# A graph network on one core: the scatter's one-hot over 128 nodes instead of 256, with messages doubled and masked by node half

## The chip, the cores and the metric

The program runs on one core of a Trainium2 chip. That core has TensorE (matmuls, with its weight loads shown apart as PEld), VectorE (DVE), ScalarE (ACT), GpSimd (POOL) and SyncE (SP), which mostly issues transfers. The metric is the device time of one execution in microseconds (us); lower is better.

## The reference

Four message-passing layers over a graph of 50,000 nodes and 50,000 edges, sorted by destination, with 64 features. Each layer gathers rows by `src` (and by `dst`), makes a message for each edge, and sums the messages into the nodes by `dst`:

```python
# layer 0: gated edges
z = concatenate([x[dst], x[src], edge_attr]); m = sigmoid(z @ W_f + b_f) * softplus(z @ W_s + b_s) * gate
out = segment_sum(m, dst) + x
# layer 1: a two-layer network on each edge
m = relu(concatenate([h[src], h[dst], e]) @ W1 + b1) @ W2 + b2;  h_new = segment_sum(m, dst)
# layer 2: two attention layers with 5 heads
out = segment_sum(a[:, :, None] * xl[src], dst).mean(heads) + bias     # a: softmax over the edges of a node
# layer 3: copied rows
agg = segment_sum(h[src], dst) * deg_in ** -0.5;  h = elu(batchnorm(agg @ W + b))
```

`deg_in` is the number of edges that end in a node. It is used by layer 3, and in the attention layers to find nodes without edges.

## The kernel before

Edges are cut into 392 tiles of 128 (one edge a partition), and four tiles make a block: `BLK = 4`, `NB = 98` blocks. Since edges are sorted by destination, the nodes of a tile nearly always lie in a window of two node tiles (`WIN = 2`, 256 nodes); the few others are left to `extra_pass`, which reads the messages back from `m_d` in DRAM.

Five stages scatter messages: `gated_edges` (names end in `_e`, from 284 to 880 us), `plain_edges` (`_e`, 1065 to 1610 us), `attention_messages` twice (`_m`, 2558 to 2898 and 4002 to 4336 us) and `copied_edges` (`_e`, 4809 to 5312 us). All use the class `NodeSums`. For a block n:

- `hot` (ScalarE, lines 933 and 938) writes a one-hot matrix of each tile: 128 edges by 256 nodes, as relu(1 - |rel - iota|). In `gated_edges` two of the four tiles are made by `match` on VectorE (line 944).
- `multiply` (TensorE, line 956) makes two products a tile, one for each node half w: a one-hot of 128 edges by 128 nodes is the stationary operand, and the messages `m`, padded with zeros from 64 to `MOVED = 128` columns, are the moving one. Each f32 product stands in the trace as two records, so a block has 16. They go to two PSUM tiles: `part_0` for tiles 0 and 1 of the block, `part_1` for 2 and 3. There is one such pair for all blocks, so the products of block n wait until VectorE has added those of block n - 1, pair by pair: `need(pe, self.added, BLK * (n - 1) + t + 2)`.
- `add` (VectorE, line 973) adds each tile's two halves to the sums in `acc`, at a tile read from `lo_i`. The windows of two tiles can overlap, so each add waits for the one before it.

The order of the work is written out by hand: each engine has a `body(n, u, i)`, and the calls in it, with their lags, are that engine's order. Blocks 0 to 5 are written out, then a loop of four blocks a turn runs. No scheduler is in between; each engine runs in order and waits at semaphores.

`attention_messages`: TensorE's body n is `project(n)` (line 2218; two halves q of a block, each 4 records, into `xl`; the two bodies share the `xl` slot of the second half) and then the scatter of block n - 2. VectorE's body n is `weigh(n)` (line 2257, two instructions of 640 elements that multiply `xl` by the attention) and then `add(n - 2)`. GpSimd sums the heads of block n in three instructions (lines 2277, 2280, 2284) and so writes `m`. ScalarE's body makes the one-hots and copies the weights `als` into `m`.

`gated_edges`: TensorE's body n is `turn(n)` (lines 1094, 1289, 1100: transposes of the gathered rows and products that pick the rows of `dst`), the scatter of block n - 2 and `project(n)` (lines 1301 to 1308). ScalarE's body n copies what `turn(n)` left (lines 1345, 1347), runs the gates of block n - 1 (lines 1353 to 1363) and its one-hots. VectorE's body n is `near.hot(n)` (line 1083, a one-hot of the other direction), `add(n - 4)`, `message(n - 2)` and `finish_message(n - 2)` (lines 1406 and 1413, which write `m`), and `match(n - 1)`.

`plain_edges` has the lags 2 for the scatter and 3 for the adds, writes `m` on VectorE (line 1617, with the bias `b1b`), and counts the in-degrees: a 65th column of ones in `m`, and a second add of two elements a tile (line 976). In these two stages and in `copied_edges` GpSimd issues one indirect gather for each tile (lines 1059, 1195, 1657), into rings of four blocks. `copied_edges` only gathers rows `z` and scatters them; its VectorE first clears the padding of `z` (line 1685) and `acc` (line 1687).

## Time and profile before

| | us |
|---|---|
| median of 3 runs | 5562.61 (5561.23 to 5564.41) |
| the profiled execution's own time | 5557.08 |
| its span in the trace | 5555.0 |
| PE busy | 4095.7 (74%) |
| PEld busy | 3075.3 (55%) |
| DVE busy | 3270.0 (59%) |
| ACT busy | 2967.9 (53%) |
| POOL busy | 3265.0 (59%) |
| granted TensorE clock, mean | 0.871 of full speed |

The program is a row of stages with a barrier after each, and each stage has its own limit, so the shares over the whole span say little. In a stage the same body runs 98 times, and what matters is the distance from one block to the next. In a view of the order of time, the first number is the start and the second how long the merged group ran; "x16" is the number of records, and the bracket tells how long the engine sat idle before and what released it.

### The profile page before, as it was taken

The numbers are of one execution on the slowest core, as the hardware profiler recorded it, in microseconds if no ns is written. First come the engines' busy times: TensorE is split into PE (matmuls) and PEld (weight loads), VectorE is DVE, ScalarE is ACT, GpSimd is POOL, SyncE is SP. The second block draws the span as 40 slices with busy tenths as digits, with TensorE's granted clock in tenths as the row PEclk, the third lists the DMA queues.
The fourth block names the chain that finished last, engine by engine and source line by source line (L and its number), as shares of the span: only waits on it lengthen the run. The fifth ranks groups of instructions, "written<-read, shape, count | busy, mean of one in ns | idle before, by whom it ended". The sixth has DMA issues, their size and how long they took to land. (4 is left out here: it accounts for less than half of the span.)

```text
span 5555.0 us, 125887 instructions
## 1 busy us (share of the span) xinstructions
PE 4095.7 (74%) x31967; PEld 3075.3 (55%) x31967; DVE 3270.0 (59%) x7378; ACT 2967.9 (53%) x7228; POOL 3265.0 (59%) x3335
## 2 busy tenths in 40 slices
PE   1079996499961999975997679999299894155574
PEld 0068885487751666653773256666177552155552
DVE  3945557588876333337879943333688799622266
ACT  0268885466655555534872234555288324755547
POOL 0876662377732655525878965554188687677710
PEclk6589998799985999987999989999699997577785
DMA  9477774755547555541334455555133334622224
GB/s 256 87 168 179 179 180 101 155 155 154 152 121 204 123 120 120 120 98 53 121 106 95 95 132 120 120 121 122 33 121 121 90 92 96 142 78 79 79 65 145
DMA packets 1204167, 680.39 MB, mean 122 GB/s; under 512 B 625921, under 2 KB 1100477, under 8 KB 1202266
## 3 DMA queue, kind: packets, MB, share of 16 engines
q1 hardware_dynamic: 1039724, 532.72, 37.1%
q0 software_dynamic: 63360, 65.01, 7.0%
q10 hardware_dynamic: 100948, 81.22, 4.6%
q8 instruction: 42, 0.69, 0.1%
q14 instruction: 93, 0.76, 0.0%
HBM read 379.93 MB, written 298.10 MB: 122 GB/s over the span
## 5 line engine op out<-in xcount | busy, mean ns | idle before, releaser
L1989 DVE COPY zT_l<-zTp_l 128x512 f32<-128x512 f32 x196 | 135.5, 691 | 899.6 <-PE alp_l L1907 650.8
L933 ACT ACTIVATE hot_e<-iota_n,rel 128x256 f32<-128x256 f32 x980 | 422.8, 499 | 418.3 <-PE part_e L956 412.4
L973 DVE TENSOR_TENSOR acc<-acc,part_e 128x128 f32 x1176 | 335.2, 285 | 467.5 <-PE part_e L956 341.7
L1964 ACT ACTIVATE leak_l<-tp_l,bcat 128x512 f32<-128x512 f32 x588 | 375.9, 686 | 433.0 <-PE tp_l L1919 404.0
L956 PE MATMUL part_e<-z_e,hot_e 128*128 128x128 f32 x1568 | 282.4, 354 | 384.0 <-DVE acc L1687 187.0
L1059 POOL DMA_INDIRECT z_l<-h_d,src_i x392 | 384.1, 980 | 288.2 <-PE zTp_l L1100 192.1
L1059 POOL DMA_INDIRECT z_l<-g_d,src_i x392 | 384.6, 981 | 287.1 <-PE zTp_l L1100 190.9
L1969 ACT ACTIVATE leak_l<-tp_l,bcat 128x256 f32<-128x256 f32 x784 | 307.7, 476 | 345.1 <-PE tp_l L1926 345.1
L1059 POOL DMA_INDIRECT z_e<-h_d,src_i x392 | 377.9, 964 | 183.8 <-issue 96.8
L956 PEld LDWEIGHTS part_e<-z_e,hot_e 128*128 128x128 f32 x1568 | 260.2, 259 | 406.1 <-DVE acc L1687 187.2
L1195 POOL DMA_INDIRECT z_e<-h_d,row_of_e x392 | 384.7, 981 | 124.6 <-issue 113.1
L1657 POOL DMA_INDIRECT z_e<-h_d,src_i x392 | 370.0, 944 | 139.9 <-issue 90.5
L956 PEld LDWEIGHTS part_m<-m_m,hot_m 128*128 128x128 f32 x3136 | 365.5, 192 | 87.9 <-DVE acc L973 80.6
L956 PE MATMUL part_e<-m_e,hot_e 128*128 128x128 f32 x3136 | 393.8, 279 | 25.7 <-DVE acc L973 21.0
L956 PE MATMUL part_m<-m_m,hot_m 128*128 128x128 f32 x3136 | 402.7, 282 | 2.3 <-ACT m_m L2243 2.0
L956 PEld LDWEIGHTS part_e<-m_e,hot_e 128*128 128x128 f32 x3136 | 372.3, 191 | 53.1 <-DVE acc L973 39.2
L933 ACT ACTIVATE hot_m<-iota_n,rel 128x256 f32<-128x256 f32 x784 | 334.3, 497 | 108.2 <-PE part_m L956 106.7
L1919 PE MATMUL tp_l<-zT_l,wcat 128*128 128x256 f32 x1176 | 372.6, 399 | 14.9 <-DVE zT_l L1989 14.9
L1919 PE MATMUL tp_l<-zT_l,wswap_l 128*128 128x256 f32 x1176 | 351.6, 381 | 0.0
L2257 DVE TENSOR_TENSOR prod_m<-xl_m,al 128x640 f32<-128x640 f32 x392 | 304.9, 819 | 32.3 <-PE xl_m L2218 19.2
L2480 DVE TENSOR_TENSOR prod_a<-xl_a,wself_a 128x640 f32<-128x640 f32 x392 | 303.6, 814 | 30.8 <-PE xl_a L2374 30.2
L2374 PE MATMUL xl_a<-wl,hT_a 64*128 64x320 f32 x1568 | 292.4, 471 | 10.8 <-DVE prod_a L2480 0.5
(419 smaller groups left out, 11050.9 us busy)
## 6 DMA issues: line engine op xcount, KB each, us to landing
m_d<-m_e ACTq DMA_DIRECT2D x196, 256.0 KB, 2.2
m_d<-m_m SPq DMA_DIRECT2D x196, 256.0 KB
h_d<-h SPq DMA_DIRECT2D x56, 448.0 KB
relb_e<-rel_d SPq DMA_DIRECT2D x196, 128.0 KB
near_e<-h_d SPq DMA_DIRECT2D x392, 64.0 KB
near_e<-g_d SPq DMA_DIRECT2D x392, 64.0 KB
relb_l<-rel_d SPq DMA_DIRECT2D x196, 128.0 KB, 3.4
near_l<-h_d SPq DMA_DIRECT2D x392, 64.0 KB
```

Of the source, the lines that this page charges most:

```text
L933: ins = self.nc.scalar.activation(self.hots[k][:, t, :], self.S["iota_n"][:, :], ACT.Abs, scale=-1.0, bias=self.S["rel"][:, ds(n * BLK + t ...
L956: mm = self.nc.tensor.matmul(self.parts[t // 2][:, t % 2, w, :], self.hots[k][:, t, w * P:(w + 1) * P], m[:, t, :], start=True, stop=True)
L973: ins = self.nc.vector.tensor_tensor(x, x, part[:, t % 2, :, 0:x.shape[2]], ALU.add)
L1059: self.nc.gpsimd.indirect_dma_start(out=self.z[n % RINGS][:, t, SIDES[t % 2]], out_offset=None, in_=self.table[0:(TILES + 1) * P, :], in_o ...
L1195: self.nc.gpsimd.indirect_dma_start(out=self.z[n % RINGS][:, t, :], out_offset=None, in_=self.source[:, :], in_offset=bass.IndirectOffsetO ...
L1657: nc.gpsimd.indirect_dma_start(out=z[k][:, t, 0:C], out_offset=None, in_=S["h_d"][0:(TILES + 1) * P, :], in_offset=bass.IndirectOffsetOnAx ...
L1919: mm = nc.tensor.matmul(by_side(tp[q])[:, side], left[:, q, :], by_side(zT[k])[:, side], start=True, stop=True)
L1964: nc.scalar.activation(leak[u % 2][:, q, :], tp[q][:, :], ACT.Relu, bias=bcat[:, 0, q:q + 1], scale=1.0 - SLOPE).then_inc(leak_ready, 1)
L1969: nc.scalar.activation(by_side(leak[u % 2][:, 3 + q, :])[:, side], tp[3 + side][:, q * 2 * P:(q + 1) * 2 * P].rearrange("p (r e) -> p r e" ...
L2257: nc.vector.tensor_tensor(heads[:, 2 * q:2 * q + 2], xl[slot(u, q)][:, :, 0:HC].rearrange("p t (h c) -> p t h c", h=H), wide(al[:, ds(n * ...
L2374: mm = nc.tensor.matmul(xl[slot(u, q)][:, half, 0:HC], hT[u % 2][rows, q * P:(q + 1) * P], wl[rows, :], start=True, stop=True)
L2480: nc.vector.tensor_tensor(prod[k][:, 2 * q:2 * q + 2, :].rearrange("p t (h c) -> p t h c", h=H), xl[slot(u, q)][:, :, 0:HC].rearrange("p t ...
```

## The change

What it does, part by part:

- The one-hots are 128 edges by 128 nodes: `rel` is reduced modulo 128 in `setup`, and `part_of` (0 or 1 for each edge and node half) is kept beside it. `hot` and `match` write half as much; `match` is one TENSOR_TENSOR of 256 elements instead of two TENSOR_SCALARs of 256. The ring of one-hots has four entries (two in `gated_edges`).
- A new VectorE instruction, `pick`, writes the messages twice, once for each node half, multiplied by `part_of`: `split`, 4 tiles x 2 x 64 = 512 elements. In `attention_messages` it does three of the four tiles (420 elements in the first layer, 414 in the second), and ScalarE does the fourth with two small instructions (`pick_too`).
- `multiply` makes one product a tile: one-hot stationary, `split` moving (128 columns; 140 and 138 in the attention layers), so 8 records a block. It waits for `picked` where it waited for `m`.
- In `attention_messages` VectorE's body n is now `pick(n - 2)`, `weigh(n)`, `add(n - 3)`. In `gated_edges` `pick(n - 2)` comes last. In `plain_edges` ScalarE writes `m` (`take`), the bias comes in by a bf16 product of 256 columns, and `pick` stands where the message was. In `copied_edges` VectorE picks block n and adds block n - 1.
- `m` has no padding: `m_d` gets 64, 69 or 70 columns a message instead of 128.
- The in-degrees ride as a 70th column of ones in the first attention layer's messages (`AW = 70`) and are copied out in `attention_nodes`; the column and the second adds of `plain_edges` are gone.
- `setup` has three more VectorE instructions for `rel` and `part_of`, and 13 more for the bias rows `b1b3`. `finish` keeps its output buffers in the unused end of `acc`.

```diff
 class NodeSums:
-        self.hots = [... sbuf_tensor(f"hot_{name}_{k}", [P, BLK, WIN * P], F32) for k in range(2)]
+        self.hots = [... sbuf_tensor(f"hot_{name}_{k}", [P, BLK, P], F32) for k in range(deep)]
+        self.split = [... sbuf_tensor(f"split_{name}_{k}", [P, BLK, WIN, width], F32) for k in range(2)]
         self.parts = [... psum_tensor(f"part_{name}_{k}", [P, 2, WIN, MOVED], F32) for k in range(2)]
...
+    def pick(self, dve, n, u, m):
+        tiles = slice(0, self.picked_first)
         need(dve, self.summed, BLK * (n - 1))
-        for t in range(self.on_act, BLK):
-            ins = self.nc.vector.tensor_scalar(self.hots[k][:, t, :], self.S["iota_n"][:, :], self.S["rel"][:, ds(n * BLK + t, 1)], None, ALU.is_equal)
-        ins.then_inc(self.matched, 1)
+        self.nc.vector.tensor_tensor(self.split[u % 2][:, tiles, :, :], wide(m[:, tiles, :], 2, WIN),
+                                     wide(self.S["part_of"][:, ds(n * BLK, self.picked_first), :], 3, self.width), ALU.mult).then_inc(self.picked, 1)
...
-    def multiply(self, pe, n, k, m):
+    def multiply(self, pe, n, u):
         need(pe, self.hot_ready, n + 1)
+        pe.wait_ge(self.picked, n + 1)
         for t in range(BLK):
             if t % 2 == 0:
                 need(pe, self.added, BLK * (n - 1) + t + 2)
...
-            for w in range(WIN):
-                mm = self.nc.tensor.matmul(self.parts[t // 2][:, t % 2, w, :], self.hots[k][:, t, w * P:(w + 1) * P], m[:, t, :],
-                                           start=True, stop=True)
+            mm = self.nc.tensor.matmul(self.parts[t // 2][:, t % 2, :, 0:self.width], self.hots[u % self.deep][:, t, :], self.split[u % 2][:, t, :, :],
+                                       start=True, stop=True)
             if t % 2:
                 mm.then_inc(self.summed, 2)
...
 def attention_messages(nc, S, g):
...
                 def body(n, u, i):
+                    if has(n, 2):
+                        pick(n - 2, u + UN - 2)
                     weigh(n, u)
-                    if has(n, 2):
-                        sums.add(dve, n - 2, sums.windows(dve, n - 2))
+                    if has(n, 3):
+                        sums.add(dve, n - 3, sums.windows(dve, n - 3))
...
 def gated_edges(nc, io, S):
...
                     if has(n, 1):
-                        sums.match(dve, n - 1, (u + 1) % 2)
+                        sums.match(dve, n - 1, u + UN - 1)
+                    if has(n, 2):
+                        pick(n - 2, u + UN - 2)
...
 def plain_edges(nc, io, S):
...
+                def take(n, u, r):
+                    act.wait_ge(mp_ready, n + 1)
+                    need(act, sums.picked, n - RINGS + 1)
+                    need(act, m_out[u % RINGS], 16 * r)
+                    nc.scalar.copy(m[u % RINGS][:, :, :], mp[u % 2][:, :, :]).then_inc(m_ready, 1)
...
 def copied_edges(nc, S):
...
-                        pool.wait_ge(sums.summed, BLK * (n - RINGS + 1))
+                        pool.wait_ge(sums.picked, n - RINGS + 1)
...
-                for k in range(RINGS):
-                    ms = nc.vector.memset(z[k][:, :, C:MOVED], 0.0)
-                ms.then_inc(s_clear, 1)
-                nc.vector.memset(S["acc"][:, :], 0.0).then_inc(s_clear, 1)
-                dve.wait_ge(s_clear, 2)
+                nc.vector.memset(S["acc"][:, 0:(TILES + 1) * C], 0.0).then_inc(s_clear, 1)
```

What stands on VectorE in body 3 of the first `attention_messages` before (`prod_m_1` is `weigh(3)`; the adds after it are block 1's, whose products TensorE makes in its own body 3):

```order
L2257 TENSOR_TENSOR prod_m_1<-xl_m_1,al 128x640
L2257 TENSOR_TENSOR prod_m_1<-xl_m_2,al 128x640
L962 TENSOR_LOAD lo_i
L973 ISA
L973 TENSOR_TENSOR acc<-acc,part_m_0 128x138
L973 ISA
L973 TENSOR_TENSOR acc<-acc,part_m_0 128x138
L973 ISA
L973 TENSOR_TENSOR acc<-acc,part_m_1 128x138
```

And after, in the same body (`split_m_1` is the pick of block 1; the adds are block 0's):

```order
L958 TENSOR_TENSOR split_m_1<-m_m_1,part_of 128x420
L2282 TENSOR_TENSOR prod_m_1<-xl_m_1,al 128x640
L2282 TENSOR_TENSOR prod_m_1<-xl_m_2,al 128x640
L986 TENSOR_LOAD lo_i
L997 ISA
L997 TENSOR_TENSOR acc<-acc,part_m_0 128x140
L997 ISA
L997 TENSOR_TENSOR acc<-acc,part_m_0 128x140
L997 ISA
L997 TENSOR_TENSOR acc<-acc,part_m_1 128x140
```

One instruction has come in ahead of the weighing, and the adds in a body are those of one block earlier.

TensorE in the same stage before, from `project(3)` to `project(4)` (`hs_m_3` and `hs_m_0`), with the products of block 1 between:

```order
L2218 MATMUL xl_m_1<-wl,hs_m_3 128x320 x2
L2218 MATMUL xl_m_2<-wl,hs_m_3 128x320 x2
L956 MATMUL part_m_0<-m_m_1,hot_m_1 128x128 x4
L956 MATMUL part_m_1<-m_m_1,hot_m_1 128x128 x4
L2218 MATMUL xl_m_0<-wl,hs_m_0 128x320 x2
```

And after:

```order
L2241 MATMUL xl_m_1<-wl,hs_m_3 128x320 x2
L2241 MATMUL xl_m_2<-wl,hs_m_3 128x320 x2
L980 MATMUL part_m_0<-split_m_1,hot_m_1 128x2x70 x2
L980 MATMUL part_m_1<-split_m_1,hot_m_1 128x2x70 x2
L2241 MATMUL xl_m_0<-wl,hs_m_0 128x320 x2
```

TensorE's order is the same, with half as many products; the scatter of block 1 still stands in body 3, ahead of `project(4)`.

## Rows read from the trace of the kernel before

**Rows 1.** Busy time in stretches: window, length, busy (records) by engine, clock, DMA, GB/s.

```profile
284.00:888.00 604.00, 552.50 (x5488) 489.30 (x5488) 330.54 (x1100) 461.80 (x1373) 382.67 (x400) 0.98 0.69 171
950.00:1046.00 96.00, 62.72 (x735) 54.85 (x735) 86.02 (x94) 72.32 (x121) 28.71 (x17) 0.95 0.97 196
...
2558.00:2900.00 342.00, 323.66 (x2352) 252.09 (x2352) 266.28 (x588) 280.52 (x588) 286.51 (x300) 0.97 0.34 113
...
4810.00:5312.00 502.00, 278.88 (x1552) 256.96 (x1552) 134.22 (x390) 268.94 (x488) 369.66 (x392) 0.76 0.29 76
```

**Rows 2.** Order of time in the first `attention_messages`, one body; start, length, instruction.

```profile
2702.22 0.74 DVE L973 TENSOR_TENSOR acc<-acc,part_m 128x138 f32 x2
...
2702.51 1.35 PE L2218 MATMUL xl_m<-wl,hs_m 64*128 64x320 f32 x8
...
2703.17 0.74 DVE L973 TENSOR_TENSOR acc<-acc,part_m 128x138 f32 x2 [0.21 <-DVE acc L973]
...
2703.79 2.05 PE L956 MATMUL part_m<-m_m,hot_m 128*128 128x128 f32 x16
2703.88 1.55 DVE L2257 TENSOR_TENSOR prod_m<-xl_m,al 128x640 f32<-128x640 f32 x2
...
2705.36 0.73 DVE L973 TENSOR_TENSOR acc<-acc,part_m 128x138 f32 x2
...
2705.77 0.54 PE L2218 MATMUL xl_m<-wl,hs_m 64*128 64x320 f32 x2
```

**Rows 3.** The same view of TensorE alone, 2702.50 to 2702.95: one half q of a projection.

```profile
2702.51 0.81 PE L2218 MATMUL xl_m<-wl,hs_m 64*128 64x320 f32 x4
```

**Rows 4.** Groups by line and shape, 2600 to 2880: busy, mean ns, idle before.

```profile
L2277 POOL TENSOR_TENSOR half_sum_m<-prod_m 128x512 f32<-128x512 f32 x86 | 109.3, 1271 | 21.2 <-DVE prod_m L2257 16.4
```

**Rows 5.** Groups by line and shape on VectorE, 12 to 30 and 480 to 720.

```profile
L431 DVE TENSOR_TENSOR square<-square 128x392 f32<-128x392 f32 x1 | 0.6, 566 | 0.0
...
L1413 DVE TENSOR_TENSOR m_e<-ln_e,sg_e 128x256 f32<-128x256 f32 x41 | 17.4, 425 | 25.4 <-ACT sg_e L1363 25.4
```

**Rows 6.** Groups by line and shape in the first `attention_nodes`, 2925 to 3185.

```profile
L2450 POOL TENSOR_TENSOR rest_a<-acc,prod_a 128x256 f32<-128x256 f32 x98 | 111.1, 1134 | 35.3 <-DVE prod_a L2480 35.3
L2485 DVE TENSOR_TENSOR half_sum_a<-prod_a 128x512 f32<-128x512 f32 x98 | 105.3, 1074 | 3.4
```

**Rows 7.** Order of time in `gated_edges`, from gates to scatter.

```profile
613.31 0.42 DVE L1413 TENSOR_TENSOR m_e<-ln_e,sg_e 128x256 f32<-128x256 f32 x1 [0.61 <-ACT sg_e L1363]
...
613.65 0.61 DVE L944 TENSOR_SCALAR hot_e<-iota_n,rel 128x256 f32<-128x256 f32 x2
...
614.22 0.88 DVE L1083 TENSOR_SCALAR hotT_e<-relb_e,iota_p 128x512 f32<-128x512 bf16 x2
...
615.04 0.72 DVE L973 TENSOR_TENSOR acc<-acc,part_e 128x128 f32 x2
...
615.81 2.09 PE L956 MATMUL part_e<-m_e,hot_e 128*128 128x128 f32 x16 [0.44 <-DVE acc L973]
...
615.97 0.72 DVE L973 TENSOR_TENSOR acc<-acc,part_e 128x128 f32 x2 [0.21 <-DVE acc L973]
...
617.73 0.38 PE L1301 MATMUL pre_e<-bias,ones 128*128 128x256 bf16 x2
```

**Rows 8.** The gathers in `plain_edges`: durations, first and last start; idle until PE: us, times.

```profile
L1195 POOL DMA_INDIRECT z_e<-h_d,row_of_e x392: 940/945/1224, 1089.4 to 1592.3; - x196
...
  PE uTp_e L1520: 6.1, 20
```

**Rows 9.** Order of time at the start of `copied_edges`.

```profile
4815.79 22.66 DVE L1687 MEMSET acc<- 128x27117 f32 x1 [5.60 <-issue]
...
4842.55 0.94 POOL L1657 DMA_INDIRECT z_e<-h_d,src_i  x1 [13.15 <-PE part_e L956]
```

**Rows 10.** Order of time in `setup`: the first and last instructions of the bias rows.

```profile
126.64 0.18 DVE L514 CAST cut_b<-bfc 3x64 bf16<-3x64 f32 x1
...
129.57 0.28 DVE L521 CAST bfc<-whole 3x256 bf16<-3x256 f32 x1
```

More of the change, by code:

```diff
@@ L53 @@
 MOVED = 128
+AW = C + H + 1
 SIDES = (slice(0, C), slice(C, 2 * C))
@@ L216, in setup @@
 def setup(nc, io, S):
-    acc, acc3, ident, ones, iota_n, iota_b = (S[k] for k in ("acc", "acc3", "ident", "ones", "iota_n", "iota_b"))
+    acc, acc3, ident, iota_n = (S[k] for k in ("acc", "acc3", "ident", "iota_n"))
     dstf, rel, src_i, dst_i, gate = (S[k] for k in ("dstf", "rel", "src_i", "dst_i", "gate"))
@@ L1310, in project @@
                     mm.then_inc(pre_ready, 1)
-                def scatter(n, u):
-                    pe.wait_ge(m_ready, n + 1)
-                    sums.multiply(pe, n, u % 2, m[u % RINGS])
                 def body(n, u, i):
@@ L1318, in body @@
                     if has(n, 2):
-                        scatter(n - 2, u + UN - 2)
+                        sums.multiply(pe, n - 2, u + UN - 2)
                     project(n, u)
@@ L1322, in _ @@
                 for n in range(NB - 2, NB):
-                    scatter(n, n)
+                    sums.multiply(pe, n, n)
             @block.scalar
@@ L1537, in degrees @@
                     mm.then_inc(counted, 1)
-                def scatter(n, u):
-                    pe.wait_ge(m_ready, n + 1)
-                    sums.multiply(pe, n, u % 2, m[u % RINGS])
                 def body(n, u, i):
@@ L1548, in body @@
                     if has(n, 2):
-                        scatter(n - 2, u + UN - 2)
+                        sums.multiply(pe, n - 2, u + UN - 2)
                 blocks(pe, body)
@@ L1553, in _ @@
                 for n in range(NB - 2, NB):
-                    scatter(n, n)
+                    sums.multiply(pe, n, n)
                 pe.wait_ge(s_zero, 1)
@@ L1571, in body @@
                     nc.scalar.activation(uT[k][:, :], uTp[k][:, 0:2 * P], ACT.Relu, bias=S["b1"][:, 0:1]).then_inc(uT_ready, 1)
+                    if has(n, 1):
+                        take(n - 1, u + UN - 1, i + (u - 1) // RINGS)
                     if has(n, 2):
@@ L1574, in _ @@
                 blocks(act, body)
-                sums.hot(act, NB - 1, 1)
+                sums.hot(act, NB - 1, NB - 1)
+                take(NB - 1, NB - 1, (NB - 1) // RINGS)
                 for n in range(NB - 2, NB):
@@ L1612, in digits, with message @@
                     ins.then_inc(lo_hi, 1)
-                def message(n, u, r):
-                    dve.wait_ge(mp_ready, n + 1)
-                    need(dve, m_out[u % RINGS], 16 * r)
-                    nc.vector.tensor_tensor(m[u % RINGS][:, :, 0:C], mp[:, :, :], wide(S["b1b"][:, :], 1, BLK), ALU.add).then_inc(m_ready, 1)
+                def message(n, u):
+                    dve.wait_ge(m_ready, n + 1)
+                    sums.pick(dve, n, u, m[u % RINGS])
                 def body(n, u, i):
@@ L2219, in project @@
                         mm.then_inc(xl_ready, 1)
-                def scatter(n, u):
-                    if isinstance(n, int) and n == 0:
-                        pe.wait_ge(s_clear, CLEARS)
-                    pe.wait_ge(m_ready, n + 1)
-                    pe.wait_ge(als_in, n + 1)
-                    sums.multiply(pe, n, u % 2, m[u % RINGS])
                 def body(n, u, i):
@@ L2244, in _ @@
                 blocks(act, body)
+                for n in range(NB - 2, NB):
+                    pick(n, n)
             @block.vector
@@ L2258, in weigh, with pick @@
                                                 wide(al[:, ds(n * BLK + 2 * q, 2), :], 3, C), ALU.mult).then_inc(weighted, 1)
+                def pick(n, u):
+                    dve.wait_ge(m_ready, n + 1)
+                    dve.wait_ge(als_in, n + 1)
+                    sums.pick(dve, n, u, m[u % RINGS])
                 def body(n, u, i):
+                    if has(n, 2):
+                        pick(n - 2, u + UN - 2)
                     weigh(n, u)
[L2262 to L2263 removed]
+                    if has(n, 3):
+                        sums.add(dve, n - 3, sums.windows(dve, n - 3))
                 blocks(dve, body)
                 for n in range(NB - 2, NB):
[L2266 removed]
+                    pick(n, n)
+                    sums.add(dve, n - 1, sums.windows(dve, n - 1))
+                sums.add(dve, NB - 1, sums.windows(dve, NB - 1))
             @block.gpsimd
             def _(pool):
[L2270 to L2271 removed]
+                if g == 0:
+                    for k in range(RINGS):
+                        nc.gpsimd.memset(m[k][:, :, C + H:AW], 1.0)
                 begin(nc.gpsimd, slice(HALF, TILES + 1), s_clear)
@@ L2534, in finish @@
         sq, e, neg = y, aT, [f[:, :, :, :].rearrange("p t h c -> p (t h c)") for f in fs]
-        xin, o = sb("xin", [P, 2 * XG, BLK * C], XS), sb("o", [P, 2, BLK, C], OR)
+        xin = sb("xin", [P, 2 * XG, BLK * C], XS)
+        past = acc[:, (TILES + 1) * C:(TILES + 1) * C + OR * W].rearrange("p (k h i c) -> p k h i c", k=OR, h=2, i=BLK)
+        o = [past[:, k] for k in range(OR)]
         aTp = [ctx.enter_context(nc.psum_tensor(f"aTp_{name}_{k}", [P, W], F32)) for k in range(2)]
```

230 lines of the change are left out of this document (127 added, 103 removed).

## The prediction

> **What bounds the kernel now.** I read it stage by stage, because the five scatter stages have different limits: first the busy time in stretches, then the order of time inside one body of each stage, to see which wait ends last.
>
> In the first `attention_messages` TensorE is busy for 324 of 342 us, at a clock of 0.97 [rows 1]. A projection starts at 2702.51, its scatter at 2703.79, the next projection at 2705.77 [rows 2]: 1.28 + 1.98 = 3.26 us a block with no gap. TensorE is the bound, but VectorE is close behind it: weighing starts at 2703.88 and the adds at 2705.36 (1.48 us), and four adds take from 2702.22 to 2703.91 (1.69 us) [rows 2]; that is 3.17 of 3.26 us.
>
> In `gated_edges` TensorE is busy for 552 of 604 us [rows 1], some 5.9 us a block once start and end are taken off, and yet a wait sets the pace: the scatter at 615.81 had waited 0.44 us for an add [rows 7], which stands behind the message, the match and hotT on VectorE.
>
> In `plain_edges` the gathers start from 1089.4 to 1592.3 us, 391 distances of 1.286 us, or 5.14 us a block, and GpSimd waited for TensorE only 6.1 us in all [rows 8]. In `copied_edges` TensorE has only 279 busy us of 502, and GpSimd issues 392 gathers [rows 1]; its one long wait is 13.15 us, before the gather at 4842.55 [rows 9]. The other 489 us are 4.99 us a block. Both stages are bound by GpSimd's gather queue.
>
> **The messages of attention.** Removed: 8 of 16 records a block, half of 1.98 us, 0.99 us. Added on VectorE: a pick of 420 elements. TENSOR_TENSORs of 256 and 392 elements take 425 and 566 ns [rows 5], 1.04 ns an element, so 420 take 0.60 us. VectorE's own work is then 3.17 + 0.60 = 3.77 us a block, above 3.26 before anything waits. That is the lower end: +0.51 us a block.
>
> The adds are also moved one body back, and this closes a ring of waits. Take the start of `weigh(n)` as 0.
> - The adds of block n - 3 start at 1.48 and end at 1.48 + 1.69 = 3.17 us [rows 2].
> - TensorE's body n has block n - 2 to scatter, whose second pair needs the last of these adds, since there is one pair of PSUM tiles. A wait for an add passes in 0.05 us (adds from 615.04 ended at 615.76, and the scatter began at 615.81 [rows 7]). Second pair: a quarter of 1.98 us and 0.1 us for a cold first record, 0.6 us. It is at 3.82.
> - `project(n + 1)` stands behind that scatter. One half of it takes 0.81 us [rows 3]: 4.63.
> - `weigh(n + 1)` waits for this half, 0.07 us more: 4.70 us, and the ring begins again.
>
> Before, the body's adds were those of block n - 2, so the scatter waited for adds of the body before and the ring had a whole body of slack. The pick falls into VectorE's new idle time, 4.70 - 3.17 = 1.53 us, and costs nothing more there.
>
> The clock: TensorE would be busy for some 2.7 us of each 4.7, 57%. A stretch with 62.7 of 96 us, 65%, had a clock of 0.95, and `copied_edges` with 279 of 502 us, 56%, but 0.76 (its slow records count longer) [rows 1]. I take 0.95; the ring has 1.4 us of TensorE in it, so 0.07 us: 4.77. At half clock throughout it would be 4.70 + 1.4 = 6.1, the upper end. With 4.77 a block costs 1.51 us more; the first three bodies of each stage are another start-up, so 95 blocks x 2 layers x 1.51 = 287 us.
>
> A port could lengthen the pick. In `attention_nodes` a VectorE add of 512 elements with both inputs in SBUF takes 1074 ns beside GpSimd's adds [rows 6], where 1.04 ns an element from [rows 5] gives 0.69, and GpSimd's own 256 elements take 1134. The pick has such inputs and runs beside GpSimd's head sums, so it may take 1.0 us; that still fits in 1.53.
>
> The Trainium skill ("SBUF — State Buffer", section "Who interferes with whom") says that a VectorE instruction with two SBUF inputs and a GpSimd one that reads SBUF block each other for a whole instruction. By that rule, the trace agrees in [rows 6] that both sides lose. If the pick met the whole of a GpSimd add of 1.27 us [rows 4], it would end at 3.17 + 1.27 + 0.60 = 5.04 us, and the ring would be 5.1 us; I keep that inside the range.
>
> **gated_edges.** The ring runs over two bodies: scatter and project, turn of the next block, ScalarE's copies and gates, VectorE's message to adds, scatter again. In it, on VectorE: the match goes from 0.61 us [rows 7] to 0.42 (256 elements [rows 5]), -0.19; the pick of 512 elements adds 0.69, less 0.08 of overlap; +0.42. On TensorE: before, the scatter took 617.73 - 615.81 = 1.92 us. After, its first pair starts as before, but its second waits for the second adds, which come 0.93 us after the first (615.97 against 615.04 [rows 7]); 0.93 + 0.6 = 1.53 us, -0.39. The sum is +0.03 us for two blocks, 2 us over 98. So the halved products come back as a wait between the pairs and as the pick ahead of the adds. Bounds: 5.14 instead of 5.9 us a block if the ring doesn't hold and the gathers become the bound as in [rows 8] (-74 us), and +0.2 (+20 us) if the pick takes 1.07 us as in [rows 6].
>
> **plain_edges.** The bound, 5.14 us of gathers a block, is not touched. At most GpSimd's 6.1 us of waiting go [rows 8]; some 2 us of clears at the start and some 2 us of shorter scatter and adds at the end. I take -8, between -10 and +10 if the new order (ScalarE's copy, then the pick) delays the turn. With half the in-degree work gone, `extra_pass` saves 1.
>
> **copied_edges.** The gathers of block 4 waited for block 0's products, which waited for the clearing of `acc`. Now they wait for block 0's pick. The clear is 25,152 elements of 27,117: 22.66 us become 21.0 [rows 9]. It ended at 4838.45; without the padding's clear it ends between 4830 and 4837, and the pick 0.7 later, against 4842.55. So -5 to -12; I take -9. The rest stays at the pace of the queue.
>
> **setup and the rest.** 13 more instructions of the kind that ran from 126.64 to 129.85 us, 3.2 us [rows 10], at the end of VectorE's list; the `part_of` ones lie in a wait for weights. +3. The write of `m` to DRAM halves; no stage waits for it. `attention_nodes` gets one copy, +1. Other stages: 0.
>
> **The sum**, against the profiled execution's own 5557.1 us: 287 + 2 - 8 - 1 - 9 + 3 + 1 = +275, 5832. The median of the runs shown is 5.5 us above that execution, so 5837 us.
>
> **Rivals.**
> - *VectorE's own work, no ring* (the products or the projection are released earlier than I read): 3.77 us a block in both attention stages. +0.51 x 190 = +97, with the other -12: 5648 us. For it: VectorE is the only engine that gains work. Against: both waits stand in the code, and the order of TensorE puts `project(n + 1)` behind the scatter.
> - *TensorE was the bound and is relieved* (other sign). In `gated_edges` the ring opens, since hotT and the match run earlier than now, and the gathers' pace decides: -74. With the attention stages at their lower end, +97, it gives 5563 - 74 - 14 + 97 = 5572. It is faster from the point where a body of VectorE takes less than 3.72 us (0.46 x 190 = 88), so with a pick of 0.55 us or less; at 0.45 us, 5543. Against: 425 ns for only 256 elements [rows 5]. [...]
> - *TensorE falls to half clock in the attention stages*: its gaps are longer than in any stage at full clock. Ring 5.5 to 6.1 us: 0.73 to 1.33 us above 4.77, x 190, 5976 to 6090. For it: the 0.76 of `copied_edges`. Against: the 0.95 at 65% [rows 1].
> - *The change does more than its ring*: a port conflict at each pick, ring 5.1, +63 more: 5900.
>
> **How the numbers follow.** The forecast's ring (4.4 to 5.1 us a block) 0.68; port or clock above it 0.14; VectorE's own work alone 0.12; relieved TensorE 0.06, half of it faster. Its own range: 4.4 gives 5765, 5.1 gives 5900. With 8 in 10 to hold, I go to 5700 below and 5930 above. A difference of 0.2%, 11 us, is what this kernel's measurements can tell from none. Faster 0.03, same 0.03, slower 0.94.
>
> **What would show it.** In the attention stages: distance of two projections 4.7 to 4.8 us instead of 3.26; VectorE's weighing idle some 0.4 to 0.9 us behind TensorE's projection, after a pick of 0.6 to 1.0; the scatter's second pair waiting for the adds; a clock of about 0.95. In `gated_edges`: 5.8 to 5.9 us a block as before, with the scatter longer than 8 records. In `plain_edges` and `copied_edges`: gathers at 5.14 and 5.0 us a block. The forecast is wrong if the attention bodies come at 3.8 us or below, or if `gated_edges` falls to 5.1 us a block.

## The result, and the profile after

The changed kernel takes 6098.49 us (median of 4 runs, 6095.35 to 6101.09) against 5561.92 us for the kernel before: ratio 1.0964, 95% interval 1.0945 to 1.0983. That is slower, as forecast, but by 537 us where I had said 275, and outside the range of 5700 to 5930.

Nearly all of it lies in the two `attention_messages` stages. The weighing on VectorE has two records a block, so from the first to the last of its 196 starts there are 97 blocks and one distance within a block, about 97.25 blocks. First the kernel before, then the changed one, both layers:

```profile
L2257 DVE TENSOR_TENSOR prod_m<-xl_m,al x196: 811/819/826, 2577.1 to 2893.4; 128x640 f32<-128x640 f32 x196
```

```profile
L2282 DVE TENSOR_TENSOR prod_m<-xl_m,al x196: 808/825/826, 2586.9 to 3162.2; 128x640 f32<-128x640 f32 x196
...
L2282 DVE TENSOR_TENSOR prod_m<-xl_m,al x196: 808/825/826, 4286.8 to 4872.3; 128x640 f32<-128x640 f32 x196
```

316.3 us became 575.3, 3.25 us a block became 5.92; in the second layer 315.4 us (4015.9 to 4331.3) became 585.5, 6.02 a block. Together +529 of the 538.6 us by which the profiled span grew (5555.0 to 6093.6). The busy time in stretches of the changed kernel, where [rows 1] showed 0.98 and 0.97 (columns as there, the engines in the order TensorE, its weight loads, VectorE, ScalarE, GpSimd, then the granted clock): `gated_edges`, then the two layers' messages.

```profile
284.00:888.00 604.00, 495.10 (x4696) 411.52 (x4696) 369.93 (x1086) 419.24 (x1373) 395.22 (x402) 0.97 0.60 150
2568.00:3166.00 598.00, 395.97 (x1552) 247.19 (x1552) 361.79 (x677) 243.87 (x782) 296.70 (x300) 0.69 0.14 45
4272.00:4876.00 604.00, 408.62 (x1552) 260.30 (x1552) 360.57 (x675) 243.78 (x782) 288.90 (x295) 0.65 0.14 44
```

TensorE has 1552 records instead of 2352, and yet is busy for 396 us instead of 324: the clock is 0.69 and 0.65. One turn of the ring in the order of time, the answer to [rows 2] (start, length, idle time before and its releaser):

```profile
2904.45 0.82 DVE L2282 TENSOR_TENSOR prod_m<-xl_m,al 128x640 f32<-128x640 f32 x1 [1.42 <-PE xl_m L2241]
2905.51 0.82 DVE L2282 TENSOR_TENSOR prod_m<-xl_m,al 128x640 f32<-128x640 f32 x1 [0.24 <-PE xl_m L2241]
...
2906.27 0.30 DVE L997 TENSOR_TENSOR acc<-acc,part_m 128x140 f32 x1
...
2907.08 0.74 PE L980 MATMUL part_m<-split_m,hot_m 128*128 128x140 f32 x4 [1.74 <-DVE acc L997]
2907.23 0.75 DVE L997 TENSOR_TENSOR acc<-acc,part_m 128x140 f32 x2 [0.21 <-DVE acc L997]
...
2907.93 1.01 DVE L958 TENSOR_TENSOR split_m<-m_m,part_of 128x420 f32<-128x420 f32 x1
2908.03 0.74 PE L980 MATMUL part_m<-split_m,hot_m 128*128 128x140 f32 x4 [0.21 <-DVE acc L997]
...
2908.71 2.12 PE L2241 MATMUL xl_m<-wl,hs_m 64*128 64x320 f32 x8
...
2909.93 0.82 DVE L2282 TENSOR_TENSOR prod_m<-xl_m,al 128x640 f32<-128x640 f32 x1 [0.98 <-PE xl_m L2241]
```

It is the ring that the prediction wrote down, link by link: weighing, the adds to 2907.98, the second pair at 2908.03, the projection at 2908.71, the next weighing at 2909.93. Only the lengths differ. The first half of the projection, 0.81 us in [rows 3], took 1.05 us here and 1.44 in the turn before:

```profile
2908.71 1.05 PE L2241 MATMUL xl_m<-wl,hs_m 64*128 64x320 f32 x4
```

```profile
2902.83 1.44 PE L2241 MATMUL xl_m<-wl,hs_m 64*128 64x320 f32 x4
```

And TensorE's clock, read in small steps over the same turn (window, length, PE busy, clock, DMA, GB/s):

```profile
2906.00:2907.00 1.00, 0.00 (x0) 1.00 0.01 1
2907.00:2908.00 1.00, 0.74 (x4) 1.00 0.00 0
...
2908.70:2909.70 1.00, 1.00 (x7) 0.73 0.00 0
2909.70:2910.80 1.10, 1.10 (x6) 0.50 0.21 68
```

In this turn the clock is at its full level (2.4 GHz) while TensorE waits, and falls to the lower one (1.2 GHz) in the course of the projection that VectorE waits for. It is not so in every turn; in the next one it is still low while TensorE waits:

```profile
2911.00:2911.50 0.50, 0.00 (x0) 0.50 0.06 18
```

Read in steps of 0.2 us from 2700 to 2900 us, the clock has a mean of 0.61 where TensorE works through the whole step and 0.82 where it waits through it. The mean of 0.69 hides that the work gets the worse part.

The groups from 2800 to 3100 us (columns as in [rows 4]):

```profile
L2241 PE MATMUL xl_m<-wl,hs_m 64*128 64x320 f32 x402 | 112.0, 700 | 0.0
L980 PE MATMUL part_m<-split_m,hot_m 128*128 128x140 f32 x404 | 94.5, 376 | 97.5 <-DVE acc L997 97.5
L2282 DVE TENSOR_TENSOR prod_m<-xl_m,al 128x640 f32<-128x640 f32 x100 | 81.4, 824 | 84.9 <-PE xl_m L2241 84.0
...
L2320 POOL TENSOR_TENSOR m_m<-half_sum_m,prod_m 128x256 f32<-128x256 f32 x51 | 43.9, 861 | 11.6 <-POOL half_sum_m L2315 10.6
```

TensorE waits for the adds (97.5 of 300 us) and the weighing for the projection (84.0): two engines that wait for each other, and none that is full.

The other stages. The gathers of `plain_edges` and `copied_edges`, the answers to [rows 8, 9]:

```profile
L1215 POOL DMA_INDIRECT z_e<-h_d,row_of_e x392: 940/947/1539, 1095.3 to 1604.4; - x196
```

```profile
L1685 POOL DMA_INDIRECT z_e<-h_d,src_i x392: 940/944/1286, 5352.9 to 5848.2; - x196
...
  DVE split_e L958: 6.9, 1
```

`plain_edges` takes 509.1 us from first to last gather instead of 502.9, `copied_edges` 495.3 instead of 501.0 (4809.7 to 5310.7), where one wait of 6.9 us stands in place of 13.15.

### The profile page after: what moved, and what is told of

The parts are those of the page before. It is cut to its first block and busy times, and to the rows that moved or that the text cites. A ratio compares the mean times of both kernels' runs of the same rounds, so it can differ in the third digit from the quotient of the medians.

```text
span 6093.6 us, 120234 instructions
## 1 busy us (share of the span) xinstructions
PE 4085.3 (67%) x28145; PEld 2861.2 (47%) x28145; DVE 3559.9 (58%) x7268; ACT 2732.4 (45%) x7718; POOL 3300.1 (54%) x3331
## 5 line engine op out<-in xcount | busy, mean ns | idle before, releaser
L980 PE MATMUL part_e<-split_e,hot_e 128*128 128x128 f32 x2352 | 463.7, 345 | 543.5 <-DVE acc L997 357.6
L980 PEld LDWEIGHTS part_e<-split_e,hot_e 128*128 128x128 f32 x2352 | 388.1, 236 | 628.2 <-DVE acc L997 418.8
L980 PE MATMUL part_m<-split_m,hot_m 128*128 128x140 f32 (+1 forms) x1568 | 381.2, 394 | 368.6 <-DVE acc L997 365.6
L980 PEld LDWEIGHTS part_m<-split_m,hot_m 128*128 128x128 f32 x1568 | 297.1, 259 | 546.6 <-DVE acc L997 525.1
L2312 POOL TENSOR_TENSOR half_sum_m<-prod_m 128x512 f32<-128x512 f32 x196 | 248.6, 1268 | 557.3 <-DVE prod_m L2282 557.3
L2282 DVE TENSOR_TENSOR prod_m<-xl_m,al 128x640 f32<-128x640 f32 x392 | 318.7, 823 | 351.1 <-PE xl_m L2241 337.8
L940 ACT ACTIVATE hot_e<-iota_n,rel 128x128 f32<-128x128 f32 x980 | 318.3, 392 | 334.3 <-PE part_e L980 294.8
L2241 PE MATMUL xl_m<-wl,hs_m 64*128 64x320 f32 x1568 | 445.4, 714 | 33.3 <-DVE prod_m L2282 24.6
L1215 POOL DMA_INDIRECT z_e<-h_d,row_of_e x392 | 390.8, 997 | 124.4 <-issue 115.9
L1685 POOL DMA_INDIRECT z_e<-h_d,src_i x392 | 370.5, 945 | 133.6 <-issue 118.9
L966 ACT ACTIVATE split_m<-m_m,part_of 128x70 f32<-128x70 f32 (+1 forms) x392 | 116.8, 345 | 707.9 <-POOL m_m L2320 696.3
```

Of the source, the lines that this page charges most:

```text
L940: ins = self.nc.scalar.activation(hot[:, t, :], self.S["iota_n"][:, 0:P], ACT.Abs, scale=-1.0, bias=self.S["rel"][:, ds(n * BLK + t, 1)])
L980: mm = self.nc.tensor.matmul(self.parts[t // 2][:, t % 2, :, 0:self.width], self.hots[u % self.deep][:, t, :], self.split[u % 2][:, t, :, ...
L1215: self.nc.gpsimd.indirect_dma_start(out=self.z[n % RINGS][:, t, :], out_offset=None, in_=self.source[:, :], in_offset=bass.IndirectOffsetO ...
L1685: nc.gpsimd.indirect_dma_start(out=z[k][:, t, :], out_offset=None, in_=S["h_d"][0:(TILES + 1) * P, :], in_offset=bass.IndirectOffsetOnAxis ...
L2241: mm = nc.tensor.matmul(xl[slot(u, q)][:, half, 0:HC], hs[u % RINGS][rows, q * P:(q + 1) * P], wl[rows, :], start=True, stop=True)
L2282: nc.vector.tensor_tensor(heads[:, 2 * q:2 * q + 2], xl[slot(u, q)][:, :, 0:HC].rearrange("p t (h c) -> p t h c", h=H), wide(al[:, ds(n * ...
```

## Experiments

All times are medians; "before" is 5558 to 5563 us in each comparison. The pace of a block is read as above, over 97.25 blocks of the first layer.

### Open the ring on VectorE's side

```
 attention_messages, vector body, behind weigh(n, u):
-    if has(n, 3):
-        sums.add(dve, n - 3, sums.windows(dve, n - 3))
+    if has(n, 2):
+        sums.add(dve, n - 2, sums.windows(dve, n - 2))
```

> Only the lag of VectorE's adds in attention_messages goes back: add(n-2) behind weigh(n) instead of add(n-3); the pick, the halved products and everything else stay. Ring theory (adds of n-3 -> second pair of the scatter of n-2 -> project(n+1) -> weigh(n+1)): the ring opens and VectorE's own work is the bound, 0.92 pick + 1.48 weighing + 1.69 adds = 4.1 us a block (3.8 to 4.2) against 5.97 now, so 190 x 1.9 less, about 5740 us (5690 to 5790), and the clock in the stage rises to 0.9 or more. Rival (the pick and its conflict with GpSimd are the price, the order is not): still 5.5 us a block or more, 6000 to 6150 us.

Measured: 5727.61 us, ratio 1.0304 [1.0287, 1.0321].

```profile
L2282 DVE TENSOR_TENSOR prod_m<-xl_m,al x196: 806/811/825, 2585.1 to 2982.7; 128x640 f32<-128x640 f32 x196
```

4.09 us a block. One lag of one body is worth 371 us. The stretch from 2700 to 2950 us shows what holds the stage now:

```profile
2700.00:2950.00 250.00, 159.76 (x972) 108.57 (x970) 209.71 (x426) 151.00 (x484) 172.76 (x183) 0.96 0.21 67
```

VectorE is busy for 210 of 250 us and TensorE for 160, at a clock of 0.96. Without the ring, the change still costs 0.84 us a block, because the pick stands on the engine that was already at 3.17 of 3.26 us.

### Open it on TensorE's side

```
 attention_messages, tensor body, behind project(n, u):
-    if has(n, 2):
-        sums.multiply(pe, n - 2, u + UN - 2)
+    if has(n, 3):
+        sums.multiply(pe, n - 3, u + UN - 3)
```

> The ring is opened on TensorE's side: body n projects block n and then scatters block n-3 instead of n-2; VectorE's order stays that of the changed kernel. Ring theory: project(n+1) no longer stands behind a product that waits for adds of the same body, so again VectorE's 4.1 us a block, about 5740 us (5690 to 5790), equal to the run with early adds within 30 us. Rival (pick and port): 6000 to 6150 us, no better than the changed kernel.

Measured: 5719.45 us, ratio 1.029 [1.0272, 1.0307]; first to last weighing 395.3 us, 4.06 a block, and the clock from 2700 to 2950 us is 1.00. VectorE's program is that of the changed kernel, pick and all. An edit on either side opens the ring, so what costs here is the circle of waits, with what it does to the clock, and not the amount of work on either engine.

### Keep TensorE busy while the ring stays

```
 attention_messages, tensor body, behind project(n, u):
+    for half in range(2):
+        for _ in range(2):
+            nc.tensor.matmul(xl[(u + 1) % 2][:, half, HC:HC + 192],
+                             S["ident"][:, :], S["iota_n"][:, 0:192], start=True, stop=True)
```

> The changed kernel with four extra products of 192 columns (8 records, about 1 us at full clock) after each projection in attention_messages, into columns that nobody reads; they stand where TensorE waits for the adds. Clock theory (the ring is 4.77 us at full clock, the rest of the 5.97 is half clock that comes of TensorE's idle time): granted clock 0.9 or more, a block 4.6 to 5.0 us, 190 x 1.1 less, about 5880 us (5830 to 5930), though TensorE has more work. Rival (the ring is longer than I counted for another reason, semaphores or the port): the clock may rise, but a block stays at 5.9 us or goes up by some of the extra products, 6080 to 6280 us.

Measured: 5878.62 us, ratio 1.0575 [1.0557, 1.0592].

```profile
2700.00:2950.00 250.00, 218.60 (x1230) 155.68 (x1229) 182.03 (x359) 127.96 (x411) 144.90 (x153) 1.00 0.18 57
```

```profile
L2285 DVE TENSOR_TENSOR prod_m<-xl_m,al x196: 814/824/826, 2584.8 to 3056.7; 128x640 f32<-128x640 f32 x196
```

Clock 1.00 and 4.85 us a block. More work on TensorE makes the kernel 220 us faster. One turn at full clock:

```profile
2801.72 1.56 DVE L2285 TENSOR_TENSOR prod_m<-xl_m,al 128x640 f32<-128x640 f32 x2 [0.72 <-POOL m_m L2323]
...
2804.95 0.74 PE L980 MATMUL part_m<-split_m,hot_m 128*128 128x140 f32 x4 [0.21 <-DVE acc L997]
...
2805.66 1.35 PE L2241 MATMUL xl_m<-wl,hs_m 64*128 64x320 f32 x8
...
2806.63 1.56 DVE L2285 TENSOR_TENSOR prod_m<-xl_m,al 128x640 f32<-128x640 f32 x2 [0.59 <-POOL m_m L2323]
```

The adds run from 2803.20 to 2804.89, so this turn is 1.48 + 1.69 + 0.06 + 0.71 second pair + 0.81 projection half + 0.16 = 4.91 us. It is the same ring: the profile names GpSimd's `m_m` as what the weighing waited for, but in the code the weighing needs the `m` of an earlier block, which the pick ahead of it had already waited for, and it starts 0.16 us behind the projection half, as in the changed kernel. The extra products end at 2803.59, ahead of the first pair of products at 2803.99, which still waits for the adds. So the ring at full clock is 4.85 us where I had worked out 4.70 to 4.77, and the rest, up to 5.92 and 6.02, is the clock.

### Cut the pick, with the ring closed

```
 attention_messages, vector pick: 8 columns of each of the three tiles instead of 70
+    nc.vector.tensor_tensor(sums.split[u % 2][:, 0:3, :, 0:8], wide(m[u % RINGS][:, 0:3, 0:8], 2, WIN),
+                            wide(S["part_of"][:, ds(n * BLK, 3), :], 3, 8), ALU.mult)
```

> VectorE's pick in attention_messages multiplies only 8 of 70 columns of each of its three tiles (48 elements instead of 420; the other columns of the products are zero, so the sums are not the reference's). Order and waits stay. Ring theory: the pick lies in VectorE's wait for the projection, so the time stays within 20 us of the changed kernel's 6098. Rival (the pick of 0.92 us is on the path, or its port conflict stretches GpSimd and so the ring): 0.6 to 0.8 us a block less, 5940 to 5990 us.

Measured: 6108.61 us, ratio 1.0991 [1.0973, 1.1009]. The pick is off the path, as said. The durations of the pick (min/median/max) are of more use; first the changed kernel with 420 elements, then this one with 48:

```profile
L958 DVE TENSOR_TENSOR split_m<-m_m,part_of x83: 596/1010/1167, 2604.5 to 3099.1; 128x420 f32<-128x420 f32 x83
```

```profile
L2291 DVE TENSOR_TENSOR split_m<-m_m,part_of x82: 208/624/781, 2603.9 to 3096.9; 128x48 f32<-128x48 f32 x82
```

The shortest pick is the 0.60 us that I had scaled from [rows 5]. The median lies 0.41 us above the shortest for 420 elements and 0.42 for 48: an addition that doesn't depend on the size. GpSimd loses too, its last add a block has a mean of 861 ns beside the large pick and 736 beside the small one. In one turn of the changed kernel the pick began first, at 2902.43, and took 0.60 us, and GpSimd's add beside it 1.17; in the next the pick took 1.01 us, and the add 0.73. That VectorE and GpSimd hold a shared pair of ports as an exclusive lock, and so wait rather than run slower, is what the Trainium skill says ("SBUF — State Buffer", section "Who interferes with whom"); the trace agrees with a wait.

### Only the lag, in the kernel before

```
 kernel before, attention_messages, vector body, behind weigh(n, u):
-    if has(n, 2):
-        sums.add(dve, n - 2, sums.windows(dve, n - 2))
+    if has(n, 3):
+        sums.add(dve, n - 3, sums.windows(dve, n - 3))
```

> The kernel before with one edit: in attention_messages VectorE's adds come one body later (add(n-3) behind weigh(n)), with the old 16 records a block and no pick. Ring theory: the ring closes here too, 1.48 weighing of the first products + 1.69 adds + 0.05 + half of the scatter, 1.0 + projection 0.81 + 0.07 = 5.1 us a block at full clock against 3.37 now; TensorE would be busy for 3.26 of 5.1 us, so the clock stays at 0.9 or a little below and I expect 5.1 to 5.5 us a block, 5920 us (5880 to 6000). Rival (the halved products and the pick are what costs, the lag of the adds alone is harmless, since a body is as long before as after): within 20 us of 5558.

Measured: 6228.22 us, ratio 1.1201 [1.1183, 1.122], well outside my 5880 to 6000. The 3.37 us a block that the expectation starts from are 3.25 in the trace, which is worth 23 us at most. The lag alone, with no pick and no halved product, costs more than the whole change. A turn of this ring:

```profile
2792.78 1.55 DVE L2257 TENSOR_TENSOR prod_m<-xl_m,al 128x640 f32<-128x640 f32 x2 [3.67 <-PE xl_m L2218]
2794.25 0.74 DVE L973 TENSOR_TENSOR acc<-acc,part_m 128x138 f32 x2
...
2795.04 3.33 PE L956 MATMUL part_m<-m_m,hot_m 128*128 128x128 f32 x16 [1.91 <-DVE acc L973]
...
2798.30 1.67 PE L2218 MATMUL xl_m<-wl,hs_m 64*128 64x320 f32 x8
2799.61 0.82 DVE L2257 TENSOR_TENSOR prod_m<-xl_m,al 128x640 f32<-128x640 f32 x1 [3.67 <-PE xl_m L2218]
```

The scatter takes 3.33 us instead of the 2.05 of [rows 2]. In small steps, its clock is 0.98 from 2795.0 to 2795.6 and 0.50 from 2795.6 to 2798.3:

```profile
2795.00:2795.60 0.60, 0.56 (x5) 0.98 0.00 0
2795.60:2798.30 2.70, 2.70 (x15) 0.50 0.43 146
```

I had repeated my own mistake here: the ring right (5.1 us), the clock taken as nearly full. The next run tests that.

### The same, kept busy

The edit is that of the run before and the four extra products of the kept-busy run together.

> The kernel before with late adds (6228 us, where I had expected 5920) and the same four idle-time products of 192 columns after each projection as in the kept-busy run; nobody reads what they write. Clock theory: the late adds' ring is 5.1 us at full clock as worked out, and 6.9 us as measured because the 1.8 us of TensorE's work in it run at half clock; kept busy it is 5.1 to 5.3 us a block, 190 x 1.65 less, about 5915 us (5880 to 5950). Rival (the ring has a wait that I have not counted): 6200 us or more.

Measured: 5958.69 us, ratio 1.072 [1.0702, 1.0738], 9 us above the upper end I gave. The clock is 1.00:

```profile
2700.00:3000.00 300.00, 277.31 (x1818) 220.46 (x1819) 150.38 (x340) 161.88 (x342) 154.44 (x171) 1.00 0.22 75
```

The weighings span 509.9 us, 5.24 a block against 6.69 with late adds alone (650.3 us). Here too the ring worked out from the rows is right to 0.14 us, and the low clock costs 1.45 us a block.

### Small picks with the ring open, in both stages

```
 NodeSums.pick, in attention_messages and gated_edges (on top of the early adds):
-    self.split[u % 2][:, tiles, :, :], wide(m[:, tiles, :], 2, WIN), ...
+    self.split[u % 2][:, tiles, :, 0:8], wide(m[:, tiles, 0:8], 2, WIN), ...
```

> The kernel with early adds (5728 us), and VectorE's pick cut to 8 columns a tile in attention_messages and in gated_edges (the other columns are zero, so the sums are not the reference's). Theory for attention_messages: with the ring open VectorE's own work is the bound, so the pick's 1.01 us (median beside GpSimd) going to 0.62 us (measured for 48 elements) takes 0.39 us off each block, 4.17 to 3.8. Theory for gated_edges: the pick (0.69 us) is in a ring over two blocks, so cutting it to about 0.25 us takes 0.22 us off a block, 22 us off the stage of 598. Together 5728 - 74 - 22 = 5630 us (5610 to 5660). Rivals: attention_messages is held by GpSimd or ScalarE and not by VectorE, no gain there (5705); gated_edges is held by its gathers or by TensorE, no gain there (5654).

Measured: 5656.84 us, ratio 1.0173 [1.0156, 1.019], 71 us below the early adds alone, where I had said 98. In `attention_messages` the weighings span 363.0 us, 3.73 a block: 0.36 less, as the pick's 0.39 said; with the ring open the pick is on the path. In `gated_edges` the messages span

```profile
L1432 DVE TENSOR_TENSOR m_e<-ln_e,sg_e x98: 424/425/471, 318.9 to 872.7; 128x256 f32<-128x256 f32 x98
```

553.8 us, 5.71 a block against 5.85 in the changed kernel (below), so 0.14 and not 0.22.

### gated_edges: pick ahead of match

```
 gated_edges, vector body:
         finish_message(n - 2, ...)
+        pick(n - 2, u + UN - 2)
     if has(n, 1):
         sums.match(dve, n - 1, u + UN - 1)
-    if has(n, 2):
-        pick(n - 2, u + UN - 2)
```

> The kernel with early adds (5728 us), and in gated_edges VectorE's pick(n-2) ahead of match(n-1) instead of behind it, so that 0.42 us of match leave the way from the message to the adds' products. Ring theory for gated_edges (two blocks a turn of the ring): 0.21 us off a block, 20 us off the stage, 5708 us. Rival (the match is then late for the adds behind it, or the stage is held elsewhere): the stage stays within 4 us of 598, 5728 us.

Measured: 5733.07 us, ratio 1.0311 [1.0294, 1.0328]; the messages go from 318.2 to 891.7, 5.91 us a block: not 20 us faster, and the 5 us above the early adds alone are within the noise. My expectation was wrong on its face. The scatter waits for the adds, and both pick and match stand ahead of the adds in either order, so nothing left that way. The trace shows one new wait: the pick now stands right behind the message that it reads, and waited for it 22 times, 5.9 us in all, where it did not wait with the match between.

```profile
  DVE m_e L1428: 5.9, 22
```

### gated_edges: adds ahead of hotT

```
 gated_edges, vector body:
-    near.hot(dve, n, u, i)
     if has(n, 4):
         sums.add(dve, n - 4, sums.windows(dve, n - 4))
+    near.hot(dve, n, u, i)
```

> The kernel with early adds (5728 us), and in gated_edges VectorE's body begins with the adds of n-4 and builds hotT behind them, instead of the other way round. The swap of pick and match could not bring the adds forward, since both stand ahead of them in either order; this one takes hotT (0.51 + 0.47 us) from ahead of the adds that the scatter waits for. Theory (ring over two blocks: message, match, pick, hotT, adds, scatter, project): up to 0.98 us off two blocks, 48 us off the stage of 598, held from below by the gathers' pace of 5.14 us a block (about 525): 5680 us (5655 to 5700). Rival (hotT then comes late for TensorE's next turn, and what the adds win the turn loses): the stage within 8 us of 598, 5728 us.

Measured: 5691.3 us, ratio 1.0231 [1.0215, 1.0246], 36 us less than with the early adds alone, where I had said 48 (within the range given). The messages in the changed kernel, then here:

```profile
L1428 DVE TENSOR_TENSOR m_e<-ln_e,sg_e x98: 424/426/486, 320.2 to 887.3; 128x256 f32<-128x256 f32 x98
```

```profile
L1428 DVE TENSOR_TENSOR m_e<-ln_e,sg_e x98: 424/426/479, 322.2 to 855.1; 128x256 f32<-128x256 f32 x98
```

5.85 us a block became 5.49. TensorE's wait for the adds from 400 to 700 us, before and behind the edit:

```profile
PE part_e L980 <- DVE acc L997: 43.1, 76, 1.4
```

```profile
PE part_e L980 <- DVE acc L997: 27.9, 68, 0.8
```

The same edit in the kernel before:

> The kernel before with the same swap in gated_edges (adds of n-4 ahead of hotT). There TensorE is busy for 288 of 300 us, so at most 12 of 300 can go: theory 10 to 24 us off the stage of 596, 5538 to 5552 us. If the halved products are what makes room, this run gains much less than the 48 us of the changed kernel. Rival (the wait for the adds is all that holds both): the same 48 us, 5514 us.

Measured: 5540.8 us, ratio 0.9962 [0.9949, 0.9975]; messages from 320.5 to 864.5, 5.61 us a block against 5.81 (315.9 to 879.9). That is 22 us, and TensorE is then full: 297.51 of 300 us. First the kernel before, then before with the swap, then the changed kernel with it:

```profile
400.00:700.00 300.00, 288.23 (x2872) 255.59 (x2871) 169.42 (x563) 241.72 (x723) 197.98 (x207) 1.00 0.71 179
```

```profile
400.00:700.00 300.00, 297.51 (x2985) 264.30 (x2982) 184.36 (x585) 249.36 (x744) 207.84 (x214) 1.00 0.73 187
```

```profile
400.00:700.00 300.00, 271.78 (x2602) 224.57 (x2598) 208.60 (x598) 231.10 (x757) 222.33 (x218) 1.00 0.68 166
```

Here the change (halved products, smaller one-hots and the pick together) does give something: 11 us more (5.49 against 5.61 a block), but only once the adds come early enough; without the swap it is 5.85 against 5.81.

### Fewer moved columns instead of fewer products

```
 kernel before, NodeSums.multiply:
-    self.parts[t // 2][:, t % 2, w, :], ..., m[:, t, :]
+    self.parts[t // 2][:, t % 2, w, 0:self.width], ..., m[:, t, 0:self.width]
```

> The kernel before with the scatter's products moving only the 64, 65 or 69 columns that are used instead of 128 (stationary one-hots as before, 16 records a block). If the moved columns set the time of a record, the scatter of a block in attention_messages falls from 1.98 to 1.07 us without any work for VectorE; the stage is then held by VectorE's 3.17 us, and gated_edges by its ring: 10 to 30 us less in all, 5530 to 5548 us. Rival (the load of 128x128 weights, 191 ns a record, or some floor of a record sets its time): within 8 us of 5558.

Measured: 5563.62 us, ratio 1.0008 [0.9998, 1.0018]; no gain. The groups from 2700 to 2800 us of the kernel before and from 2750 to 2850 us of this run:

```profile
L956 PE MATMUL part_m<-m_m,hot_m 128*128 128x128 f32 x495 | 63.5, 281 | 0.0
```

```profile
L956 PE MATMUL part_m<-m_m,hot_m 128*128 128x69 f32 x496 | 62.1, 278 | 0.0
...
L956 PEld LDWEIGHTS part_m<-m_m,hot_m 128*128 128x128 f32 x496 | 57.7, 191 | 13.6 <-DVE acc L973 13.6
```

With 69 columns a record takes what it took with 128, while the loads of 128x128 weights keep their 191 ns. So the moved columns don't set a record's time in this range; what does, the load or something else, no run isolates. One product of 140 columns costs about what one of 128 did, but halving their number does not quite halve the scatter: with early adds, at full clock, the next projection begins 1.15 us behind the scatter's start (2801.29 to 2802.44), against 1.98 in the kernel before.

### The mixture

The changed kernel with `attention_messages` as in the kernel before (two products a tile, no pick, adds of n - 2) and `gated_edges` with the adds first:

```
 attention_messages:
-    sums = NodeSums(nc, S, ctx, name, WIDTH, picks_on_act=1)
+    sums = WholeSums(nc, S, ctx, name, WIDTH)      # the NodeSums of the kernel before
+    # rel_full = rel + P * part_of[:, :, 1], since rel is now modulo 128
 ...
```

> The changed kernel with attention_messages put back to the two products a tile of the kernel before (16 records a block, no pick, adds of n-2), and with gated_edges' adds ahead of hotT. Theory: attention_messages is back at 3.35 to 3.4 us a block, 527 us less than 6098, and the other stages of the change are neutral (5571 us); gated_edges gives 48 us more: 5523 us (5495 to 5540), below the kernel before. Rival (the halved products of gated_edges have no slack to give): 5571 us, 10 above the kernel before.

Measured: 5527.96 us, ratio 0.9939 [0.9926, 0.9953]. It beats both kernels, by 35 us the one before, and is 13 us below the kernel before with the swap. The messages of `gated_edges` go from 319.3 to 852.2, 5.49 us a block again; the weighings of the first `attention_messages` span 317.0 us, 3.26 a block, against 316.3 and 3.25 in the kernel before.

## Why the prediction was wrong, point by point

- **The ring of `attention_messages`.** Right: each wait stands in the trace in the order given, and it opens from either side. At full clock it is 4.85 us against my 4.70 to 4.77: the second pair took 0.71 and not 0.6, and the weighing started 0.16 behind the projection half and not 0.07. Of the 2.67 us that a block of the first layer gained, 0.84 are there without a ring, 0.76 come of the ring at full clock, and 1.07 of the clock; the forecast had 1.51 for all three.
- **The clock.** This is the step that failed: "I take 0.95; the ring has 1.4 us of TensorE in it, so 0.07 us: 4.77." Measured: 0.69 and 0.65 in the mean, and down to 0.50 within the projection, so that a turn takes 5.92 and 6.02 us on average. With the four extra products the clock was 1.00 and 220 us went. Two faults lie in that step. I set two busy shares side by side, 65% and 57%, although the second row named in the same sentence, `copied_edges` with 56% and 0.76, was the nearer one; and a busy share at the lower clock contains records that last longer, so it isn't comparable. And I multiplied a mean clock into the ring. Even the measured mean would have given too little that way, 1.4 / 0.69 - 1.4 = 0.63 us and a ring of 5.3: the clock was lower where TensorE worked (0.61) than where it waited (0.82). What sets the level in a given turn stays open.
- **The low clock also reaches VectorE.** The first projection half is not all: in the turn shown the second weighing waited 0.24 us for the second half, so the adds begin 1.82 us behind the first weighing, not 1.48. For the turn shown: 1.82 + 1.71 adds + 0.05 + 0.68 second pair + 1.05 projection half + 0.17 = 5.48 us.
- **The rival** with TensorE at half clock gave a ring of 5.5 to 6.1 us and 5976 to 6090 us; that is what happened, 8 us beyond its end. I gave port and clock together 0.14, and cut the range at 5930, which left this rival out although its price was known.
- **The pick.** 0.60 us alone and 1.0 beside GpSimd, as worked out from [rows 5, 6], and hidden in the wait while the ring is closed.
- **VectorE's own work.** With the ring open 4.09 us a block, 3.17 + 0.92, and the pick has a mean of 0.89 us there. The rival's 3.77 took it at 0.60.
- **gated_edges.** Forecast +2; measured (887.3 - 320.2) - (879.9 - 315.9) = +3.1 us. As said, TensorE's saved records came back as its wait for the adds, 43.1 us instead of 11.8 in the 300 us from 400 to 700, so the sum held. The block before was 5.81 us and not the 5.9 that the bound of -74 started from. Not all links held: the small pick gave 0.14 us a block where the ring asked for 0.22.
- **plain_edges.** Forecast -8, measured +6.2. The gathers' bound is touched: the 392 gathers were busy for 390.8 us instead of 384.7. Whether the picks beside them do that was not tested; in `copied_edges`, where picks run beside the gathers too, the 392 gathers took 370.5 us against 370.0.
- **copied_edges.** Forecast -9, measured -5.7. The wait went from 13.15 to 6.9 us, the clear from 22.66 to 21.0 us as worked out.
- **setup.** The first message of `gated_edges` is at 320.2 instead of 315.9, +4.3 against +3.

## What to carry to other kernels

Before a wait is moved by one body, write down which engine's next step stands behind the work that waits; a lag that looks like slack can close a ring, and here it cost 371 us of 537, the lower clock included. Price TensorE's part of any new ring at the lower clock as well as at the full one, and keep that end in the range: here the engine that was relieved and then waited ended up slower at its own work. In `gated_edges` the relief of the fullest engine paid only once the wait beside it was shorter: the order of two calls gave 22 us, and the change 11 more.

## What the runs showed of the hardware that was not expected

- Products that nobody reads made a kernel faster: 6098 to 5879 us, and with late adds 6228 to 5959 us, at a clock of 1.00. The Trainium skill ("TensorE: Matmul & The Clock Gate", section "Part 1: The HAM clock gate (the "warmup" mystery)") calls the low clock the default that activity releases; these two runs agree.
- A wait of TensorE does not by itself lower the clock. With early adds it waited 1.58 us in one body, in turns of 4.1 us, and kept a clock of 0.96 over 250 us. With the ring closed it waited 1.74 us (at 2907.08, above), in turns of 5.9 us, and the clock fell to 0.50 in the projection that followed. The wait with early adds:

```profile
2801.29 1.22 PE L980 MATMUL part_m<-split_m,hot_m 128*128 128x140 f32 x8 [1.58 <-DVE split_m L958]
```

- An f32 product against 128x128 weights takes the same time with 69 and 128 moved columns (means of 278 and 281 ns a record), and about the same with 140 (the shortest took 282 ns, against 275 with 128).
- A VectorE multiply with two SBUF inputs beside GpSimd's adds took 0.41 us longer in the median than at its shortest, whether it has 48 or 420 elements.
